# Row maxima of the first unit in two halves, each with its own row transfer

## The reference

```
q, k, v = x @ w_q, x @ w_k, x @ w_v                 # per head
logits  = q @ k.T / sqrt(64)        (causal mask)
probs   = softmax(logits)
x = layernorm(x + (probs @ v) @ w_o)
x = layernorm(x + ffn(x))
```

## Time and profile before

| | |
|---|---|
| median of three runs | 1036.18 us |
| the profiled execution | 1035.9 us |
| its span | 1034.2 us |
| TensorE busy | 1007.0 us, 97% |
| VectorE busy | 778.0 us, 75% |
| GpSimd busy | 750.9 us, 73% |
| ScalarE busy | 613.1 us, 59% |

### The profile page before, as it was taken

How to read it: one execution, slowest core, us unless ns; L and a number is a source line. 1 busy time by engine, 2 the same in 40 slices (tenths; PEclk the granted TensorE clock), 3 DMA queues, 4 the chain that set the end, 5 groups by cost and what they waited for, 6 DMA issues and landing times.

```text
span 1034.2 us, 17742 instructions
## 1 busy us (share of the span) xinstructions
PE 1007.0 (97%) x5816; PEld 697.7 (67%) x5816; DVE 778.0 (75%) x2112; ACT 613.1 (59%) x1246; POOL 750.9 (73%) x715
## 2 busy tenths in 40 slices
PE   6799999999999999999999999999999999999997
PEld 4566676676666776676666766767666766765687
DVE  7767777877777777878788778877778888785356
ACT  3555656566656656666556656666555656665544
POOL 6567887777768887777778877777778887777510
PEclk8899999999999999999999999999999999999999
DMA  6233122233222222232232222332222222320002
GB/s 190 62 83 82 45 72 53 62 83 83 58 68 62 63 65 60 63 83 63 70 76 58 62 56 55 83 83 63 66 60 74 63 57 57 83 64 22 22 11 73
DMA packets 48602, 68.71 MB, mean 66 GB/s; under 512 B 15191, under 2 KB 25083, under 8 KB 48510
## 3 DMA queue, kind: packets, MB, share of 16 engines
q1 hardware_dynamic: 48510, 67.57, 25.3%
HBM read 31.11 MB, written 2.36 MB: 32 GB/s over the span
## 4 chain that ended last, share of the span: by engine, by line
PE 92%; DVE 3%; DMA 2%; ACT 1%; issue 1%; POOL 0%; SPq 0%; POOLq 0%; ACTq 0%
PE O L717 25%; PE WORK L631 14%; PE SC L692 14%; PE SC L696 13%; PE WORK L644 6%; PE WORK L679 3%; PE WORK L607 3%; PE WORK L609 3%; PE WORK L608 3%; PE WORK L772 2%; PE WORK L617 1%; PE WORK L619 1%; PE WORK L618 1%; DVE WORK L991 1%; DMA R<-RROW 1%
## 5 line engine op out<-in xcount | busy, mean ns | idle before, releaser
L863 ACT ACTIVATE PR<-SC 128x512 f32<-128x512 f32 (+3 forms) x768 | 352.3, 490 | 263.9 <-PE SC L696 231.4
L519 POOL TENSOR_TENSOR SUM<-SUM,PR 128x1024 f32<-128x1024 f32 (+3 forms) x256 | 419.0, 1637 | 14.8 <-POOL SUM L528 0.5
L991 DVE CUSTOM_DVE_ANT_0 WORK<-WORK,CMASK 128x128 f32<-128x128 f32 (+3 forms) x512 | 239.3, 514 | 65.7 <-PE WORK L631 65.6
L692 PE MATMUL SC<-QH,KHL 128*128 128x512 f32 (+3 forms) x768 | 268.8, 356 | 3.1 <-ACT PR L863 3.0
L696 PE MATMUL SC<-QL,KH 128*128 128x512 f32 (+3 forms) x768 | 261.7, 346 | 3.3 <-DMA QL<-NROW 3.3
L504 POOL TENSOR_SCALAR_AFFINE_SELECT PR<-PR 128x256 f32<-128x256 f32 x256 | 105.9, 415 | 198.0 <-ACT PR L863 197.9
L631 PE MATMUL WORK<-KHL,QH 128*128 128x512 f32 (+3 forms) x768 | 226.5, 365 | 5.9 <-DMA KH<-KHL 4.1
L717 PE MATMUL O<-PR,VLO 128*64 128x512 f32 (+3 forms) x1024 | 200.0, 522 | 0.3 <-DVE OT L1075 0.3
L692 PEld LDWEIGHTS SC<-QH,KHL 128*128 128x128 f32 x768 | 145.2, 189 | 60.7 <-ACT PR L863 28.5
L631 PEld LDWEIGHTS WORK<-KHL,QH 128*128 128x128 f32 x768 | 136.7, 191 | 59.3 <-issue 35.4
L994 DVE TENSOR_REDUCE MP<-WORK 128x1 f32<-128x512 f32 x256 | 164.1, 684 | 4.8
(11 more groups left out here) (132 smaller groups left out, 1099.0 us busy)
## 6 DMA issues: line engine op xcount, KB each, us to landing
QH<-QH SPq DMA_DIRECT2D x128, 128.0 KB, 2.4
KH<-KHL SPq DMA_DIRECT2D x128, 128.0 KB, 2.3
R<-RROW SPq DMA_DIRECT2D x64, 256.0 KB, 3.8
SW<-in_L_ffn_up_weights_dram SPq DMA_DIRECT2D x9, 512.0 KB, 4.4
SW<-_L_ffn_down_weights_dram SPq DMA_DIRECT2D x9, 512.0 KB, 4.3
out_dram<-X SPq DMA_DIRECT2D x7, 256.0 KB, 2.3
X<-in_L_attn_x_BSE_dram SPq DMA_DIRECT2D x3, 512.0 KB, 4.5
X<-in_L_attn_x_BSE_dram SPq DMA_DIRECT2D x2, 256.0 KB, 3.3
```

The costliest lines, as they stand in the source:

```text
L519: nc.gpsimd.tensor_tensor(total, total, prob(unit, s), ALU.add).then_inc(add_done, 1)
L692: nc.tensor.matmul(dst, KHL[:, par, h, kt * P:(kt + 1) * P], QH[:, par, h, q0:q0 + n], start=True, stop=False)
L863: nc.scalar.activation(prob(unit, s)[:, h, :], SC[use % NSC][:, 0:n], ACT.Exp, scale=K ** -0.5).then_inc(exp_done, 1)
L991: op = nc.vector.tensor_tensor_reduce(cols, cols, CMASK[:, CH - n:], 1.0, LOWEST, ALU.add, ALU.max, cell)
```

## The change

The first unit's maxima are made in two parts. `PREFETCH` keeps the six maxima of the first query chunk, which now stand ahead of the second key chunk's projection; the key projection of the first chunk moves ahead of the values. The other fifteen become work steps `("first", i)` of unit 0's own steps 0 to 3: six in step 0, four in step 1, three in step 2, two in step 3. After each part VectorE makes the reduce and the four transposes, and SP sends that half by two transfers of four rows each (`first_rows`), one per head. The first part's transfers stand where `rows(0)` stood on SP's queue; the second part's stand behind the duplicates of unit 1. TensorE waits for the first part ahead of L696 of step 0 and for the second ahead of L696 of step 4. Later units keep their single transfer, with other counts on the semaphores.

```diff
--- before.py
+++ after.py
@@ -128,10 +128,15 @@
 W1_SPLIT_AT = (UNITS - 1, 8)
 
 
+FIRST_MAXES = [(s, place, ("first", i)) for i, (s, place) in enumerate(
+    [(0, BETWEEN)] * 3 + [(0, BEHIND)] * 3 + [(1, BETWEEN)] * 4 + [(2, BETWEEN)] * 3 + [(3, BETWEEN)] * 2, CHUNK0_MAXES)]
+assert FIRST_MAXES[-1][2][1] == len(MAXES) - 1
+
+
 def unit_fillers(u):
 
     b, n = u // PAIRS, u % PAIRS
-    rows = []
+    rows = list(FIRST_MAXES) if u == 0 else []
     for s, place, f in FILLERS:
         if f[0] == "norm":
             missing = u < 1
@@ -152,7 +157,8 @@
     return sorted(rows, key=lambda row: row[:2])
 
 
-PREFETCH = [("proj", 0, 0), ("v", 0), ("proj", 1, 0), ("proj", 0, 1), ("v", 1), ("proj", 1, 1)] + MAXES + [("proj", 0, 0)]
+PREFETCH = [("proj", 0, 0), ("proj", 1, 0), ("v", 0), ("proj", 0, 1)] + MAXES[:CHUNK0_MAXES]
+PREFETCH += [("proj", 1, 1), ("v", 1), ("proj", 0, 0)]
 SCHEDULE, NUMBER, n = [], {}, len(PREFETCH)
 for u in range(UNITS):
     SCHEDULE.append([])
@@ -352,6 +358,10 @@
             n = CH - START[s] if n is None else n
             return PR[:, (unit * NS + s) % PRING, :, 0:n]
 
+        def rows_landed(unit):
+
+            return 64 + 16 * unit
+
         block = ctx.enter_context(nc.Block())
 
 
@@ -400,10 +410,18 @@
                         sp.dma_start(KH1[A, par, h, cols].bitcast(F32), KHL[half, par, h, cols].bitcast(F32))\
                             .then_inc(dup_landed[c], 16)
 
+            def first_rows(c):
+
+                sp.wait_ge(nrow_made, c + 1)
+                for h in range(2):
+                    dst = QL[K:K + 1, 0, h, c * CH:(c + 1) * CH].rearrange("a (t c) -> a t c", t=TPC)
+                    row = h * TILES + c * TPC
+                    sp.dma_start(dst.bitcast(F32), NROW[row:row + TPC, :].bitcast(F32)).then_inc(m_landed, 16)
+
             def rows(unit):
 
                 par = unit % 2
-                sp.wait_ge(nrow_made, (unit + 1))
+                sp.wait_ge(nrow_made, unit + 2)
                 dst = QL[K:K + 1, par, :, :].rearrange("a h (t c) -> a (h t) c", t=TILES)
                 sp.dma_start(dst.bitcast(F32), NROW[0:2 * TILES, :].bitcast(F32)).then_inc(m_landed, 16)
 
@@ -429,10 +447,12 @@
             sp.dma_start(BROW, BLOCKS).then_inc(brow_in, 16)
             sp.dma_start(W1[:, :], W_exp).then_inc(in_exp, 16)
             sp.dma_start(X[:, TILES:2 * TILES, :], x_tiles[:, TILES:2 * TILES, :]).then_inc(in_x[2], 16)
-            rows(0)
+            first_rows(0)
             for u in range(UNITS):
                 if u + 1 < UNITS:
                     copies(u + 1)
+                if u == 0:
+                    first_rows(1)
                 if u < 2:
                     sp.dma_start(X[:, (u + 2) * TILES:(u + 3) * TILES, :],
                                  x_tiles[:, (u + 2) * TILES:(u + 3) * TILES, :]).then_inc(in_x[u + 3], 16)
@@ -444,7 +464,7 @@
                     if STAGE_UNIT[n] - 1 == u:
                         stage_weights(n)
             inverses(UNITS - 1)
-            sp.wait_ge(m_landed, 16 * UNITS)
+            sp.wait_ge(m_landed, rows_landed(UNITS - 1))
             for c in range(CHUNKS):
                 sp.wait_ge(dup_landed[c], 64 * UNITS)
 
@@ -617,9 +637,14 @@
                         nc.tensor.matmul(out, XTH[:, lo:lo + P], WSV[:, 0, :], start=True, stop=False)
                         nc.tensor.matmul(out, XTH[:, lo:lo + P], WSV[:, 1, :], start=False, stop=False)
                         t = nc.tensor.matmul(out, XTL[:, lo:lo + P], WSV[:, 0, :], start=False, stop=True)
-                elif f[0] == "max":
-                    pieces = f[1]
-                    unit, nxt = u + 1, (u + 1) % 2
+                elif f[0] in ("max", "first"):
+                    pieces = f[1] if f[0] == "max" else MAXES[f[1]][1]
+                    unit = u + (f[0] == "max")
+                    nxt = unit % 2
+                    if f == ("first", CHUNK0_MAXES):
+                        evacuated(NUMBER[-1, ("proj", 0, 1)])
+                        evacuated(NUMBER[-1, ("proj", 1, 1)])
+                        pe.wait_ge(dup_landed[1], 64)
                     for c in range(CHUNKS):
                         if f == MAXES[c * CHUNK0_MAXES]:
                             evacuated(NUMBER[u - (c == 0), ("proj", 0, c)])
@@ -691,8 +716,10 @@
                     pe.wait_ge(exp_done, unit * 2 * NS + use + 1)
                     nc.tensor.matmul(dst, KHL[:, par, h, kt * P:(kt + 1) * P], QH[:, par, h, q0:q0 + n],
                                      start=True, stop=False)
-                    if s == 0 and h == 0:
-                        pe.wait_ge(m_landed, (unit + 1) * 16)
+                    if (unit, s, h) == (0, 0, 0):
+                        pe.wait_ge(m_landed, 32)
+                    elif (s, h) == (0, 0) or (unit, s, h) == (0, FIRST_OF[1], 0):
+                        pe.wait_ge(m_landed, rows_landed(unit))
                     nc.tensor.matmul(dst, KH1[:, par, h, kt * P:(kt + 1) * P], QL[:, par, h, q0:q0 + n],
                                      start=False, stop=True).then_inc(scores_ready, 1)
                     if h == 0:
@@ -821,7 +848,7 @@
             def evacuate(u, f, at):
 
                 w, free = WORK[at % NWORK], work_free[at % NWORK]
-                if f[0] in ("max", "out", "w2", "wo", "con", "bias"):
+                if f[0] in ("max", "first", "out", "w2", "wo", "con", "bias"):
                     return
                 act.wait_ge(work_ready, at + 1)
                 if f[0] == "x1":
@@ -993,13 +1020,16 @@
                         else:
                             op = nc.vector.tensor_reduce(cell, cols, AX_X, ALU.max)
                     op.then_inc(free, 1)
-                    if f == MAXES[-1]:
+                    if f == MAXES[-1] or (u < 0 and f == MAXES[CHUNK0_MAXES - 1]) or f == ("first", len(MAXES) - 1):
+                        made = 0 if u < 0 else 1 if f[0] == "first" else u + 2
                         dve.wait_ge(free, at // NWORK + 1)
                         nc.vector.tensor_reduce(NEGM[:, 0:2 * TILES], MP[:, :, :], AX_X, ALU.max,
                                                 negate=True).then_inc(negm_made, 1)
-                        dve.wait_ge(negm_made, u + 2)
-                        if u >= 0:
-                            dve.wait_ge(m_landed, (u + 1) * 16)
+                        dve.wait_ge(negm_made, made + 1)
+                        if made == 1:
+                            dve.wait_ge(m_landed, 32)
+                        elif made > 1:
+                            dve.wait_ge(m_landed, rows_landed(u))
                         for b in range(0, P, BLK):
                             op = nc.vector.transpose(NROW[:, b:b + BLK], NEGM[b:b + BLK, :])
                         op.then_inc(nrow_made, 1)
```

## The result

The changed kernel takes 1045.19 us (median of five runs, 1044.13 to 1047.21) against 1035.88 us of the kernel before (1035.47 to 1036.36): a ratio of 1.0092, 95% interval 1.0078 to 1.0105. It is 9.3 us slower. The forecast was slower by 4.6 us, 1040.8, in a range up to 1043.0: the sign and the place held, the size did not. The profiled execution took 1044.13 us, with a span of 1042.4 against 1034.2, so 8.2 us are there to be read.

A forecast was written before the change was run, and what follows sets the result against it. TensorE was taken as the bound, with room only in the opening: step 4 4.9 us later, 0.86 returned (4.0 left), 0.6 added for clock, so +4.6 on 1035.9 and 0.3 to the median: 1040.8 us, range 1037.3 to 1043.0.

The forecast's parts named there:

- Part 3: VectorE's work before step 4: 16.8 us from 29.1 to 45.9, rows landing at 48.3, step 4 4.9 us later.
- Part 4: Behind step 4's wait: 0.86 us bank wait given back, 0.6 us added for TensorE's half clock; sum +4.6 us.
- Part 1: New opening: maxima start at 15.15 us, first rows made at 19.8, second keys' ScalarE copies at 19.5, VectorE done at 25.9.
- What bounds the kernel: TensorE, nearly always busy from 45.17 us on; a microsecond won or lost ahead of 45 us reaches the end nearly whole.
- the point of comparison: Second matmul (L696) of unit 0's step 4, same TensorE steps ahead in both kernels: 43.45 us before, 48.3 forecast.
- Part 2: SP's queue: first rows, ready at 19.8 us, issued behind loads at 24.4 and 25.0, landing at 28.2.
- The 0.86 us: TensorE's idle piece before 45.17 us in the kernel before, waiting for VectorE to free a bank; forecast to fall away.
- C: Rival, worse, about 1043.4 us: low-weight subtraction meets GpSimd's addition (+1.5), clock falls for its full 2.4 us (+0.6); chance 0.11.
- B: Rival, faster, about 1035.1 us: VectorE hardly idles from 15.15 us to the second transposes; chance 0.10.
- point of decision: 3.1 us of idle VectorE between 15 and 46 us puts step 4 at 44.3; below it the change wins.

The follow-up runs named there:

- the runs with TensorE kept busy: Changed kernel with the high-part matmul repeated ahead of the waits for rows: in both waits 1043.82 us (1.0080), in step 4's wait alone 1044.44 us (1.0079).
- the rows ahead of the loads: Changed kernel with the first half's two row transfers moved ahead of the seven loads on SP's queue: 1040.03 us, ratio 1.0048.
- TensorE busy in both waits: Changed kernel with the high-part matmul ahead of the wait made 18 times in step 0 and 15 times in step 4: 1043.82 us, ratio 1.0080.
- the move with the old projections: Changed kernel with projections and values in the order of the kernel before, split and fifteen moved maxima kept: 1038.93 us, ratio 1.0038.
- the split alone: Kernel before with rows made and sent in two halves, all 21 maxima and the projections left in the prefetch: 1031.19 us, ratio 0.9962.

## Why the prediction was right in kind and wrong in size

**The step that failed** is the price of TensorE's half clock behind the two waits. The forecast put 0.2 us on it behind the first rows (Part 3) and 0.6 behind the second (Part 4); the stretches of the changed kernel against those of the runs with TensorE kept busy show 1.8 and 1.7. The value matmuls came 4.1 us later than forecast: 2.7 of it are this price, 1.6 are Part 1's delay (1.1) and the landing of the first rows (0.55), and 0.3 more was given back than I had. The mechanism, VectorE's work in front of step 4 and a second transfer that TensorE waits for, is the one forecast.

**What bounds the kernel, and the point of comparison:** right. From the first value matmuls on, all kernels take 981.4 to 983.1 us, so a loss in the opening goes through whole.

**Part 1** ended 1.0 us late: the second keys' copies on ScalarE were over at 20.5 us, not 19.5. Half of it is the landing of the first key duplicates, for which I took the time from issue to use of before (2.96 us): VectorE idled 0.66 us until 15.68. With the keys' projection moved forward they are issued while a weight load still runs (the last is issued at 7.80 us and takes 4.7 to land), and reached TensorE 3.1 to 5.0 us after issue in the profiles (11.76 to 14.88, 10.95 to 15.95). The other half is the second key projection: the third maximum ended at 17.43 and its result was read out by 17.57, TensorE began at 17.70 and ended its third matmul at 19.27, 1.7 us after the bank was free, where I had 1.4 (16.9 to 18.3).

**Part 2**, the queue: right as a mechanism, shown by the rows ahead of the loads (-4.6 us by the ratios), too small in size. Issue came at 25.5 instead of 24.4, which is Part 1's delay; the landing took 3.66 us from the second issue, where I had taken 3.2 from a 2 KB transfer whose issue had three loads fewer ahead of it; in two other profiles the rows were used 5.0 and 5.3 us after the first issue (26.02 to 31.04, 25.77 to 31.09). The sentence by the Trainium skill (DMA: Bandwidth & Descriptors, Two DMAs through the same engine are not ordered) asked for the landing of the 512 KB load ahead; the trace agrees with its direction only: the rows were used at 29.86, past its 28.5, and no view here shows which descriptors waited for which.

**Part 3**, VectorE's order: the terms from 36.4 us on (12.8 us, forecast 12.65) and the two transfers (2.4) were right. Ahead of it, from the first rows to unit 1's key subtraction, I had 5.05 us (28.2 to 33.25) and it took 6.54 (29.86 to 36.40). TensorE ran at the half clock through this stretch, and I had put 0.2 us on that; at full clock the same stretch took 4.73 (31.09 to 35.82, TensorE busy in both waits). Part 1, Part 2 and this give the 3.3 us by which step 4 was late: 1.1 + 0.55 + 1.5, and 0.15 in VectorE's later terms.

**Part 4**, what is given back. I had +0.6 for the clock; the two runs with TensorE kept busy show 1.7. Before, the half clock lasted 2.4 us; here it lasted most of 3.9. The upper end of 1.2 was also too low, since I took the one stretch of before for the longest there can be. The sentence by the page TensorE: Matmul & The Clock Gate (Trainium skill, Part 1: The HAM clock gate) pointed to the higher value, and these runs agree with it for this wait. The 0.86 us was given back as forecast, and 0.3 more with it (8.56 - 0.86 - 7.42). So the stretch from step 4 to the value matmuls was 9.09 against the 8.3 in my sum (8.56 - 0.86 + 0.6), 0.8 more. With the 3.3 of step 4 that makes 4.1 us at 60.67; 0.5 of it came back later, and what is left is the profile's 8.2 against the forecast 4.6.

**The range** failed for a plain reason: four terms were each bounded by the one row of before that was nearest, and all of them (landing, round trip, two stretches at the half clock) went the same way at once. I had counted on "not all at once". That a late landing brings idleness, idleness the half clock and the half clock longer waits is my reading; the rows show the parts, and no run the whole chain. The remaining 1.1 us between the profile's 8.2 and the medians' 9.3 is the spread of the changed kernel's runs, 3.1 us against 0.9. The landing of the first key duplicates, 14.9 to 16.3 us among the profiles with keys first, is a likely source; it was not tried apart.

**The rivals:** C was nearest in kind, with the clock but without its other half, the slow subtraction beside GpSimd (0.42 us at 44.04 us here, ahead of GpSimd's addition at 45.50). B's point of decision, 3.1 us of idle VectorE between 15 and 46 us, was borne out from the other side: VectorE was idle for 10.9 us from 15.02 to 49.18 us in the changed kernel (busy 23.3 of 34.2), and for 5.5 from 15.02 to 44.08 us in the move with the old projections (23.5 of 29.1), and both are slower than before.

## What to carry to other kernels

Split a result's hand-over where its parts are used at different times, but leave the work that makes it where its engine is free: the split alone gave 4.0 us, and moving the fifteen maxima behind the first use cost 7.9. Before a transfer or a wait is placed on an in-order queue, list what is queued ahead of it and behind it at the new time: twice in these runs one row transfer's place was worth 3 to 5 us. When a change makes a matmul engine wait, add the slower clock behind the wait to its price, and bound terms that feed each other together. And look at what runs beside a short operation: the same subtraction took 0.42 us or 1.9, and its place beside GpSimd's addition decided it.
